# A Strassen-split AdaLN + routed low-rank FFN: both tiles' routed factors turned on VectorE, and the pair's order rearranged around it

## What is computed

```python
x1 = einsum('bct,bcd->bdt', x, weights[condition])
result = einsum('bnd,od->bno', x1, W_base) + b_base
logits = einsum('bnd,ed->bne', x1, W_gate)
# softmax, the two highest of eight, renormalised: route_w
h = einsum('bnd,erd->bner', x1, A)
delta = einsum('bner,eor->bno', h * route_w[..., None], B)
out = x + result + delta            # SCALING is 1
```

## Time and profile before

| | us |
|---|---|
| median of 3 runs | 943.2 (943.04 to 944.24) |
| the profiled execution, its own time | 942.72 |
| its span, first to last instruction | 941.0 |
| PE busy | 935.8 (99%) |
| DVE / ACT / POOL busy | 525.5 / 384.4 / 535.8 |
| granted TensorE clock | 1.00 in all slices |

### The profile page before, as it was taken

The page is one execution under the profiler, slowest core; times in us unless marked ns, Lnnn a source line. Parts: engine busy times, 40 slices in busy tenths (PEclk is TensorE's granted clock), DMA queues, the critical chain, the costliest instruction groups (busy, mean ns, idle before and its releaser), DMA issues.

```text
span 941.0 us, 17296 instructions
## 1 busy us (share of the span) xinstructions
PE 935.8 (99%) x5444; PEld 880.9 (94%) x5444; DVE 525.5 (56%) x1808; ACT 384.4 (41%) x810; POOL 535.8 (57%) x506
## 2 busy tenths in 40 slices
PE   9999999999999999999999999999999999999998
PEld 7899999999999999999999999999999999999997
DVE  5785555545555455555555554555555555555554
ACT  6463343434334334444334344333443343434332
POOL 3575546655566555575555665555655547555560
PEclk9999999999999999999999999999999999999999
DMA  9522332233322233322333223333223332233312
GB/s 306 187 79 101 134 115 98 89 111 123 134 92 92 95 123 134 111 99 91 108 126 127 95 86 104 123 134 105 87 89 120 134 112 100 89 111 123 134 45 90
DMA packets 41453, 107.13 MB, mean 114 GB/s; under 512 B 4450, under 2 KB 8675, under 8 KB 41443
## 3 DMA queue, kind: packets, MB, share of 16 engines
q1 hardware_dynamic: 41440, 107.01, 32.9%
q10 hardware_dynamic: 2, 0.00, 0.0%
HBM read 73.43 MB, written 33.55 MB: 114 GB/s over the span
## 4 chain that ended last, share of the span: by engine, by line
PE 98%; DVE 1%; DMA 0%; ACT 0%; issue 0%; SPq 0%; DVEq 0%
PE ps L816 54%; PE ps_r L816 19%; PE ps_out L834 11%; PE ps_out L844 10%; PE ps L875 2%; PE ps L886 1%; DVE w_sum L615 1%; PE ps_r L875 1%; DMA raw<-in_x_t 0%; PE ps_hwt L840 0%; ACT a_hi L418 0%; PE ps_r L861 0%; PE ps L861 0%; PE ps L834 0%; DVE o_sb L652 0%; PE ps L844 0%
## 5 line engine op out<-in xcount | busy, mean ns | idle before, releaser
L316 POOL TENSOR_TENSOR a_lo<-raw,a_hi 128x512 fp32r<-128x512 f32 x128 | 165.9, 1318 | 245.1 <-ACT a_hi L418 245.1
L816 PE MATMUL ps<-w_hi,s_hi 128*128 128x448 f32 x480 | 177.6, 370 | 0.0
L816 PE MATMUL ps<-w_lo,s_hi 128*128 128x448 f32 x480 | 175.5, 366 | 0.0
L816 PE MATMUL ps<-w_hi,s_lo 128*128 128x448 f32 x480 | 173.6, 362 | 0.0
L632 DVE TENSOR_TENSOR z_sum<-ps,z_sum 128x448 f32<-128x448 f32 x150 | 93.7, 625 | 128.5 <-PE ps L816 128.3
L816 PE MATMUL ps_r<-r_hi,a_hi 128*128 128x264 f32 x496 | 140.7, 284 | 0.0
L816 PE MATMUL ps_r<-r_hi,a_lo 128*128 128x264 f32 x496 | 140.7, 284 | 0.0
L816 PE MATMUL ps_r<-r_lo,a_hi 128*128 128x264 f32 x496 | 140.6, 284 | 0.0
L652 DVE TENSOR_TENSOR o_sb<-ps_out,o_sb 128x312 f32<-128x312 f32 (+1 forms) x190 | 93.1, 505 | 76.8 <-PE ps_out L844 76.7
L816 PE MATMUL ps<-w_hi,a_hi 128*128 128x448 f32 x360 | 131.9, 367 | 0.0
L816 PE MATMUL ps<-w_hi,a_lo 128*128 128x448 f32 x360 | 130.6, 363 | 0.0
(11 more groups left out here) (135 smaller groups left out, 1711.3 us busy)
## 6 DMA issues: line engine op xcount, KB each, us to landing
raw<-in_x_t SPq DMA_DIRECT2D x128, 256.0 KB, 2.7
o_sb<-in_x SPq DMA_DIRECT2D x64, 512.0 KB, 3.6
out_x<-o_sb SPq DMA_DIRECT2D x62, 512.0 KB, 2.6
w_sum<-in_w_t SPq DMA_DIRECT2D x8, 448.0 KB, 9.2
r_raw<-in_w_t SPq DMA_DIRECT2D x4, 264.0 KB, 5.7
table_raw<-in_cond_w SPq DMA_DIRECT2D x2, 256.0 KB, 8.8
b_raw<-in_b_t SPq DMA_DIRECT2D x1, 512.0 KB, 10.8
out_x<-o_sb SPq DMA_DIRECT2D x2, 224.0 KB, 2.1
```

The costliest lines, as they stand in the source:

```text
L316: pool.tensor_tensor(a_lo[j][:], raw[j][:], as_f32(a_hi[j][:]), ALU.subtract).then_inc(s_a_lo[j], 1)
L816: mm = pe.matmul(bank[:, 0:w.shape[-1]], a[:, k, :], w[:, k, :], start=(opens and k == 0 and q == 0), stop=(closes and k == KH - 1 and q = ...
```

## The change

- `hw` of tile a is transposed by DVE too, in the loop: 16 blocks, in four parts of four (one 32-partition stripe of the result each), set between the other DVE work from P5 to the end of P3. Its `hwt_top` and `hwt_rest` read SBUF. TensorE's transposes stay for pairs 0, 1 and 31 (`pe_hwt_top`).
- Tile b's piece L is mixed behind the next step's P1 instead of in front of the end of R; its ranking, weighing and the 16 transposes move to the head of the next step on DVE. ACT's copy of P1 waits for that mix.
- On PE tile b's low rank moves behind tile a's R product, tile a's low rank to the very end of the step, and the mix of b's Q and R behind P6.
- ACT and POOL are reordered to suit (`s_rest` of S4 ahead of tile b's mix tile).
- In `first()`, DVE's sum T3 moves behind `hwt_rest(1)`, and T1's remainder behind `hwt_rest(2)`.
- SP loads the bias ahead of B22.

```diff
 # sync, start of the program
             load_w("B12")
+            for c in range(3):
+                sp.dma_start(bias[:, at[c]:at[c] + BASE_COLS[c]],
+                             b_base[:, base(c)].to_broadcast([P, BASE_COLS[c]])).then_inc(s_bias_in, 16)
             load_w("B22")
             for j in (A11, A21, A22):
                 sp.wait_ge(s_a_lo[j], 1)
                 load_raw(1, j)
-            for c in range(3):
-                sp.dma_start(bias[:, at[c]:at[c] + BASE_COLS[c]],
-                             b_base[:, base(c)].to_broadcast([P, BASE_COLS[c]])).then_inc(s_bias_in, 16)
 # gpsimd, step
                 fetch_mix(p, 0)
+                s_rest(p, 4, raw[A12][:], s2_hi, s2_lo)
                 pool.wait_ge(s_mixed[1][R], p)
                 fetch_mix(p, 1)
-                s_rest(p, 4, raw[A12][:], s2_hi, s2_lo)
 # scalar, step
                 act.wait_ge(s_p[1], p + 1)
+                act.wait_ge(s_mixed[1][L], p)
                 act.copy(z_sum[1][:, cols(L)], ps_1[:, 0:NS]).then_inc(s_p1_out, 1)
-                turned_hwt_top(p - 1)
+                exps(2 * p - 1)
                 act.wait_ge(s_p[6], p + 1)
                 sum_top(p, 4, raw[A12][:], s2_hi)
+                hwt_top(2 * p - 1)
...
                 added_top(p, 0, Q)
-                seed(p, 1, L)
+                hwt_top(2 * p)
                 sum_top(p + 1, 2, s2[:], s2_hi)
-                exps(2 * p + 1)
                 act.wait_ge(s_r_sum[1], p + 1)
                 z_top(1, R, ps_r[:, 0:width[R]])
+                a_top(p + 1, A21)
+                a_top(p + 1, A22)
+                seed(p, 1, L)
                 seed(p, 1, R)
                 seed(p, 1, Q)
-                a_top(p + 1, A21)
-                a_top(p + 1, A22)
 # vector, end of the preamble and first()
             t_sum(1, T1, T3, T1)
-            dve.wait_ge(s_w0_lo["B12"], 2)
-            t_sum(3, T3, T2, T3)
             def first():
                 z_rest(1, 0, L, ps_1[:, 0:NS])
                 hwt_rest(1)
+                dve.wait_ge(s_w0_lo["B12"], 2)
+                t_sum(3, T3, T2, T3)
 # vector, step
             def step(p, last):
+                rank_experts(p - 1, 1)
+                weigh_experts(p - 1, 1)
+                turn_hw(2 * p - 1)
                 dve.wait_ge(s_p1_out, p - 1)
                 dve.wait_ge(s_p[6], p + 1)
                 add(ps_6, p1, u2).then_inc(s_u2, 1)
                 hwt_rest(2 * p - 1, hwt_sum[:])
...
                 weigh_experts(p, 0)
+                if not last:
+                    turn_hw(2 * p, (0,))
                 dve.wait_ge(s_p[5], p + 1)
                 dve.wait_ge(s_u3, p - 1)
                 add(ps_5, u3, u3).then_inc(s_z_sum[1, Q], 1)
+                if not last:
+                    turn_hw(2 * p, (1,))
                 added_rest(p, 1, Q)
+                if not last:
+                    turn_hw(2 * p, (2,))
                 dve.wait_ge(s_p[4], p + 1)
                 add(ps_6, p1, p1).then_inc(s_z_sum[1, L], 1)
-                added_rest(p, 1, L)
-                hwt_rest(2 * p)
                 dve.wait_ge(s_p[3], p + 1)
                 dve.wait_ge(s_u2, p - 1)
                 add(ps_5, u2, u2).then_inc(s_z_sum[0, Q], 1)
...
-                output(p, 0, L)
+                turn_hw(2 * p, (3,))
                 added_rest(p, 0, Q)
-                output(p, 0, R)
-                rank_experts(p, 1)
+                hwt_rest(2 * p, hwt_sum[:])
+                added_rest(p, 1, L)
                 z_rest(p, 1, R, ps_r[:, 0:width[R]])
+                output(p, 0, L)
+                output(p, 0, R)
                 output(p, 0, Q)
-                weigh_experts(p, 1)
-                turn_hw(2 * p + 1)
 # tensor, step
                 strassen(ps_1, a_hi[A11], a_lo[A11], B11, True).then_inc(s_p[1], 1)
-                mix_chunk(p - 1, 1, Q)
-                mix_chunk(p - 1, 1, R)
+                mix_chunk(p - 1, 1, L)
                 pe.wait_ge(s_s_lo[2], p - 1)
                 strassen(ps_6, s2_hi, s2_lo, T2, True).then_inc(s_p[6], 1)
+                mix_chunk(p - 1, 1, Q)
+                mix_chunk(p - 1, 1, R)
...
-                strassen(ps_5, s2_hi, s2_lo, B22, False, lambda: turn_hw(2 * p)).then_inc(s_p[3], 1)
+                if last:
+                    strassen(ps_5, s2_hi, s2_lo, B22, False, lambda: turn_hw(2 * p)).then_inc(s_p[3], 1)
+                    mix_chunk(p, 1, L, ps_6)
+                else:
+                    strassen(ps_5, s2_hi, s2_lo, B22, False).then_inc(s_p[3], 1)
+                pe.wait_ge(s_a_lo[A21], p + 1)
+                plain_r(ps_r, 1, 0, True, False)
+                if not last:
+                    plain_r(ps_r, 1, 1, False, True).then_inc(s_r_sum[1], 1)
+                mix_chunk(p, 0, Q)
                 pe.wait_ge(s_hwt_lo, 2 * p + 1)
                 lora(0, L)
                 lora(0, R)
-                if last:
-                    mix_chunk(p, 1, L, ps_6)
-                pe.wait_ge(s_a_lo[A21], p + 1)
-                plain_r(ps_r, 1, 0, True, False)
-                if not last:
-                    mix_chunk(p, 1, L)
-                    plain_r(ps_r, 1, 1, False, True).then_inc(s_r_sum[1], 1)
-                mix_chunk(p, 0, Q)
                 lora(0, Q)
```

More of the change, by code:

```diff
@@ L496, in _ @@
             a_top(1, A11)
-            hwt_top(1)
+            pe_hwt_top(1)
             act.wait_ge(s_p[3], 1)
@@ L513, in first @@
                 z_top(0, L, ps_1[:, 0:NS])
-                hwt_top(2)
+                pe_hwt_top(2)
                 t_top(1, T1)
@@ L526, in first @@
                 z_top(0, R, ps_r[:, 0:width[R]])
-                hwt_top(3)
+                pe_hwt_top(3)
                 t_top(4, NT4)
@@ L557, in step @@
                 z_top(0, R, ps_r[:, 0:width[R]])
+                if not last:
+                    a_top(p + 1, A11)
+                seed(p, 0, L)
+                if not last:
+                    a_top(p + 1, A12)
                 seed(p, 0, R)
                 seed(p, 0, Q)
-                if not last:
-                    a_top(p + 1, A11)
                 exps(2 * p)
-                if not last:
-                    a_top(p + 1, A12)
-                    sum_top(p + 1, 3, s3[:], s3_hi)
+                if last:
+                    finish(p)
+                    return
@@ L566, in step @@
+                sum_top(p + 1, 3, s3[:], s3_hi)
                 added_top(p, 1, Q)
-                if not last:
-                    sum_top(p + 1, 1, s1[:], s1_hi)
+                sum_top(p + 1, 1, s1[:], s1_hi)
                 added_top(p, 1, L)
-                if last:
-                    act.copy(ps_6[:, 0:NS], bias[:, cols(L)]).then_inc(s_seed[L], 1)
-                hwt_top(p + 2)
                 added_top(p, 0, Q)
-                if last:
-                    act.wait_ge(s_z_lo[0][L], p + 1)
-                    act.copy(ps_1[:, 0:NS], bias[:, cols(Q)]).then_inc(s_seed[Q], 1)
-                    exps(2 * p + 1)
-                    seed(p, 1, R)
-                    return
@@ L580, in step, with finish @@
-                seed(p, 1, L)
+                hwt_top(2 * p)
                 sum_top(p + 1, 2, s2[:], s2_hi)
-                exps(2 * p + 1)
                 act.wait_ge(s_r_sum[1], p + 1)
                 z_top(1, R, ps_r[:, 0:width[R]])
+                a_top(p + 1, A21)
+                a_top(p + 1, A22)
+                seed(p, 1, L)
                 seed(p, 1, R)
                 seed(p, 1, Q)
-                a_top(p + 1, A21)
-                a_top(p + 1, A22)
+            def finish(p):
+                act.wait_ge(s_z_lo[0][L], p + 1)
+                act.copy(ps_1[:, 0:NS], bias[:, cols(Q)]).then_inc(s_seed[Q], 1)
+                added_top(p, 1, Q)
+                added_top(p, 1, L)
+                act.copy(ps_6[:, 0:NS], bias[:, cols(L)]).then_inc(s_seed[L], 1)
+                pe_hwt_top(4)
+                added_top(p, 0, Q)
+                exps(2 * p + 1)
+                seed(p, 1, R)
+                pe_hwt_top(5)
+                act.wait_ge(s_r_sum[1], p + 1)
+                z_top(1, R, ps_r[:, 0:width[R]])
@@ L636, in _, with turn_hw @@
             u3 = z_sum[1][:, cols(Q)]
-            def turn_hw(i):
+            def turn_hw(i, parts=range(P // TURN)):
                 dve.wait_ge(s_hw, i + 1)
-                for c in range(P // TURN):
+                for c in parts:
                     for r in range(P // TURN):
@@ L727, in first @@
                 hwt_rest(1)
+                dve.wait_ge(s_w0_lo["B12"], 2)
+                t_sum(3, T3, T2, T3)
+                for c in (L, Q, R):
+                    output(0, 1, c)
                 dve.wait_ge(s_t_sum[1], 1)
@@ L744, in first @@
                 hwt_rest(2)
+                t_rest(1, T1)
                 dve.wait_ge(s_t_sum[3], 1)
@@ L784, in step @@
                     return
+                turn_hw(2 * p, (3,))
+                added_rest(p, 0, Q)
+                hwt_rest(2 * p, hwt_sum[:])
```

(10 more changed lines are left out.)

37 lines of the change are left out of this document (11 added, 26 removed).

## The result

The changed kernel takes 979.39 us (median of 4 runs, 979.35 to 980.01) against 943.12 for the kernel before (median of 4, 942.76 to 944.24): a ratio of 1.0383, 95% interval 1.0370 to 1.0395. It is 36.3 us slower. The execution that is profiled took 979.4 us, with a span of 977.4 (before: 942.72 and 941.0), at a granted clock of 1.0, as before.

A forecast was written before the change was run, and what follows sets the result against it. PE, 99% busy, was taken to bound the kernel. 942.72 - 3.2 + 41.5 - 0.3 + 0.2 = 980.9 us for the profiled execution, 0.5 more for the median: 981.4, eight-in-ten range 943.5 to 985.

The forecast's parts named there:

- PE's transpose: In each of the 29 loop steps TensorE no longer transposes tile a: 0.11 us less, -3.2 us in all.
- first wait: Per loop step, PE waits 0.74 us at the mix of Q, because z_lo stands behind GpSimd's S4.
- second wait: Per loop step, PE waits 0.69 us at tile a's low rank, because hwt_lo stands behind GpSimd's remainder of S2.
- start: Before the loop, bias ahead of B22 and T3's sum later: -0.3 us for both, between +0.6 and -0.7.
- last step: In the last step PE asks for tile a's Q 2.06 us after P3, there at 2.09 + 0.16: +0.2 us.
- The margin: After P3, z_lo asks 0.11 us behind S4, if both ends of the part are spaced as transposes are.
- The price: Step's end: late DVE row ends at POOL's end + own length - 0.13, late POOL row 1.15 us after DVE's.
- Every step starts its clock anew at P3, so nothing heals: In the loop no step makes up for its waits, so both count 29 times: +41.5 us.
- The head of the step: Tile b's L work on DVE at the step's start costs nothing, with two us of cover before PE needs it.
- Rival 1: After P3, z_lo asks before S4: 0.15 to 0.37 us a step, 944.2 to 950.6 us; chance 0.18.
- Rival 2: Per step only the first wait, as hwt_rest goes ahead of S2's remainder: 21.5 us, 961.4 in all; chance 0.10.
- Rival 3: In the loop transposes are free, exclusion hardly touches 448- and 128-column rows, no microsecond wait: 939.9 us; chance 0.16.

The follow-up runs named there:

- experiment 6: Changed kernel, but TensorE transposes tile a's hw again, in the middle of P3: 942.27 us, ratio 0.9990 to the kernel before.
- experiment 2: Changed kernel, but GpSimd's S4 waits in the loop until tile a's remainder of Q (z_lo) is done: 940.10 us, ratio 0.9965.
- experiment 5: Changed kernel, but GpSimd's remainder of S2 waits in the loop for tile a's hwt_lo: 961.2 us, ratio 1.0190.
- experiment 1: Changed kernel, but one of the four transposes ahead of tile a's remainder of Q is made before P4's add: 943.33 us, ratio 1.0002.
- pool_waits_again: The kernel of experiment 2 measured once more, unchanged: 940.21 us, ratio 0.9969 to the kernel before.

## Why the prediction was right, point by point

981.4 was predicted, by two waits per step, and 979.4 measured. By the terms of the sum:

| term | predicted | measured |
|---|---|---|
| PE's transpose, per step | -0.11 | -0.09 (28.89 in experiment 6, 28.81 in 2) |
| first wait, per step | +0.74 | +0.69 (experiment 5) |
| second wait, per step | +0.69 | +0.68 (the rest of 1.37) |
| 29 steps, all three | +38.3 | +37.4 |
| start | -0.3 | about -0.9 |
| last step | +0.2 | about +0.1 |

- *The margin.* It all hung on z_lo asking 0.11 us behind S4; it was 0.12. The step that decided was to give the part of four the 0.03 us at both ends that transposes show among themselves. The trace agrees: the add ends at 392.98 and the block starts at 393.02, the last block ends at 393.94 and z_lo starts at 393.97. With rows overlapping by 0.08 at both ends z_lo would have asked first. The Trainium skill, VectorE: DVE Perf Modes, section "Two Vector instructions with no wait between them", has a model by which an instruction whose operands start in other 32-partition quadrants than the last ones starts only when every earlier one has finished. By it both ends of the part are held (the part writes in the last quadrant, the rows around it in the first), and the trace agrees: 0.04 and 0.03 us. (The prediction says that without this rule the sum would be that of the second rival; it means the first, where the remainder wins.)
- *The price.* "POOL's end, own length, less 0.13" gave z_lo's end as 3.48 after P3 and hwt_lo's as 4.78; in the trace they are 3.46 and 4.76 (395.54 + 1.38 less 392.16). "1.15 behind DVE's end" gave 4.63 for the remainder of S2; it is 4.61. Both constants came from DVE rows of 1792 columns and hold for those of 448 and 128. The Trainium skill, SBUF — State Buffer, section "Who interferes with whom", says that a Vector instruction with two SBUF inputs contends with a GpSimd instruction that reads SBUF, and that the order of issue decides who blocks. The rows agree: z_lo takes 1.65 us as the second and 0.63 as the first.
- *The first wait* was 0.05 too long by two roundings: z_lo ends at 3.46 instead of 3.48, and R's matmuls lie 0.12 apart, so that PE, whose last one starts at 394.97, wants the mix at 2.93 and not at 2.90.
- *"Every step starts its clock anew at P3, so nothing heals"* held: the steps in the loop are 30.17 to 30.19 us long.
- *The head of the step* cost nothing, as forecast: PE has no further wait in the loop.
- *The start* was undersized, outside my own -0.7: I priced T3's sum by one PE wait (at most 0.45) and did not cost T1's remainder, which the diff also moves. The traces show 0.45 for the sum, 0.24 for the remainder and 0.2 to 0.45 for the bias.
- *Rival 1* (the remainder wins, 944.2 to 950.6) is what happens in experiment 1's kernel: steps of 28.92, 943.3 us, a little under its range. It was 0.2 us on one engine away. *Rival 2* (only the first wait, 961.4) has the price of experiment 5's, 961.2, but there a semaphore keeps GpSimd back. Its own reason, that DVE goes first with two instructions of its own, is refuted by the changed kernel: the remainder of S2 asks at 395.10 while z_lo runs until 395.62, and goes ahead of hwt_lo. *Rival 3* (faster, 939.9) is what the change is worth when nobody loses a race: 940.1 in experiment 2. Its reason, that 448-column rows hardly exclude, is wrong; its sum is right partly by luck, since PE's saving was 0.7 us smaller and the start 0.6 better.
- *The sum and the ranges.* 981.4 is 2.0 too high: about 0.9 by the loop, 0.6 by the start, 0.1 by the last step, and 0.5 that I added to get from the profiled execution to the median, where the two are now the same (979.4). Two bounds don't follow from their own words. Each wait by 0.08 either way is 29 x 0.16 = 4.6, so 976.8 to 986.0 and not 976 to 985; and 943.5 lies below rival 1's 944.2, not in the middle of its lower half. The outcome doesn't hang on either.

What stays open: which of the two goes first when they ask within less than 0.05 us of each other, which no step shown here had.

## What to carry to other kernels

Where VectorE and GpSimd both have instructions with two SBUF inputs near a point at which they are released together, write down when each asks, since in the rows shown here the first one kept its length and the other paid for it. Work inserted in this kernel cost next to nothing while it left z_lo first (experiment 1), and 36 us as soon as it didn't. Give the race to the one that TensorE waits for by a semaphore on the engine that has slack, instead of leaving it to 0.1 us: here a wait of 1.00 us per step on GpSimd was worth 39 us in all. An order on a third engine (ScalarE's casts) decides such a race as well, so what releases each of the two belongs in the account.

## What was not expected of the hardware

- Two casts exchanged on ScalarE moved the time from 948.5 to 976.0 us, through nothing but the order in which VectorE and GpSimd asked.
- The margin is finer than a transpose. In experiment 2 VectorE's z_lo of tile b asked at 410.22 and S4 at 410.27, both while hwt_lo ran until 410.31, and 0.05 us were enough: z_lo kept 0.62, S4 took 1.73 and ended 1.16 behind it.
- A busy share says little here: the changed kernel's DVE is busy for 728.3 us, that of experiment 2 for 646.1 (the page of `pool_waits_again`) with the same 2272 instructions. The 82 us between them are waits that the rows count as work.
